# Placing in a sort kernel: the tile one-hot held still while both halves of the values stream past it

## What is computed

```
edge_index = jnp.stack([src, dst])
h = jnp.maximum(_layernorm(x, axis=-1), 0.0)
x = x + _L0_gnn_ref(h, edge_index, L0_gnn_kernel, L0_gnn_bias)
h = jnp.maximum(_layernorm(x, axis=-1), 0.0)
x = x + _L1_gnn_ref(h, edge_index, Wq, bq, Wk, bk, Wv, bv, gamma, beta)
# layer 0: sums = segment_sum(h[dst], by src); relu([mean, h] @ kernel + bias)
# layer 1: softmax attention of 8 heads over the edges of each src, then a layer norm
```

## Time and profile before

| what | us |
|---|---|
| median of 3 runs | 4550.31 |
| lowest and highest | 4537.21, 4554.0 |
| span of the profiled execution | 5884.4 |
| POOL busy, 55% of the span | 3217.7 |
| PE busy, 52% | 3071.8 |
| DVE busy, 52% | 3038.8 |
| ACT busy, 36% | 2089.2 |

### The profile page before, as it was taken

The page is one execution under the profiler, slowest core; times in us unless marked ns, Lnnn a source line. Parts: engine busy times, 40 slices in busy tenths (PEclk is TensorE's granted clock), DMA queues, the critical chain, the costliest instruction groups (busy, mean ns, idle before and its releaser), DMA issues. The chain is left out here.

```text
span 5884.4 us, 82972 instructions
## 1 busy us (share of the span) xinstructions
PE 3071.8 (52%) x19417; PEld 2269.0 (39%) x19417; DVE 3038.8 (52%) x8517; ACT 2089.2 (36%) x6025; POOL 3217.7 (55%) x3339
## 2 busy tenths in 40 slices
PE   4445445445445455354357555555555555555553
PEld 3324323334334333233234444444444444444442
DVE  7536446445345455354234555555555555555557
ACT  3233333433433333333344333333333333333333
POOL 3464464464564564554634555655555555555564
PEclk9556556556556556566557666666666666666665
DMA  2232232232222322322322333333333333333333
GB/s 80 63 82 53 70 80 55 73 79 55 76 72 56 81 68 57 84 62 61 87 57 68 101 103 100 106 101 102 104 101 105 102 101 105 101 104 103 100 105 63
DMA packets 245464, 490.01 MB, mean 83 GB/s; under 512 B 73156, under 2 KB 155197, under 8 KB 245022
## 3 DMA queue, kind: packets, MB, share of 16 engines
q0 software_dynamic: 153968, 371.50, 24.5%
q1 hardware_dynamic: 90350, 112.89, 6.9%
q10 hardware_dynamic: 704, 0.33, 0.0%
HBM read 468.15 MB, written 56.11 MB: 89 GB/s over the span
## 5 line engine op out<-in xcount | busy, mean ns | idle before, releaser
L533 POOL DMA_INDIRECT got<-hk_table,dst x1563 | 1561.2, 999 | 1325.5 <-PE bank L1003 647.5
L1513 POOL DMA_INDIRECT kv<-kv_table,dst_i x1611 | 1523.0, 945 | 1062.8 <-DVE wv_s L1554 611.4
L765 DVE TENSOR_TENSOR acc<-acc,bank 128x129 f32 x2187 | 634.2, 290 | 1250.2 <-remote 640.9
L1001 PE MATMUL bank<-got,oh 128*128 x2187 | 609.3, 280 | 1170.6 <-DVE acc L765 627.0
L1658 PE MATMUL bank<-q,ohT 128*128 x4833 | 757.8, 263 | 878.4 <-issue 574.6
L1572 DVE TENSOR_TENSOR acc<-acc,bank 128x136 f32 x1611 | 465.4, 289 | 1130.0 <-remote 1070.7
L1669 PE MATMUL bank<-wv_s,oh_f 128*128 128x136 f32 x3222 | 806.6, 401 | 255.5 <-issue 251.1
L1658 PEld LDWEIGHTS bank<-q,ohT 128*128 128x128 bf16 x4833 | 487.9, 101 | 1124.5 <-issue 1018.6
L1104 ACT ACTIVATE oh<-away 128x384 bf16<-128x384 bf16 x733 | 383.1, 523 | 1321.9 <-remote 784.1
L1669 PEld LDWEIGHTS bank<-wv_s,oh_f 128*128 128x128 f32 x3222 | 660.0, 282 | 344.0 <-issue 336.1
L1001 PEld LDWEIGHTS bank<-got,oh 128*128 128x128 bf16 x2187 | 239.9, 110 | 1369.2 <-issue 1317.5
(11 more groups left out here) (223 smaller groups left out, 3344.4 us busy)
## 6 DMA issues: line engine op xcount, KB each, us to landing
lane_r<-lane_of_slot SPq DMA_DIRECT2D x269, 192.0 KB
slots_by_bin<-sorted_chunk SPq DMA_DIRECT2D x637, 61.0 KB
kv<-kv_table,dst_i POOLq DMA_INDIRECT x1611
got<-hk_table,dst POOLq DMA_INDIRECT x1563
kv_table<-qkv SPq DMA_DIRECT2D x12, 512.0 KB, 2.9
hk_table<-hk POOLq DMA_DIRECT2D x6, 772.0 KB, 5.3
out<-o SPq DMA_DIRECT2D x12, 256.0 KB
xs<-in_x SPq DMA_DIRECT2D x3, 768.0 KB, 9.7
```

The source lines that it names most:

```text
L533: g.indirect_dma_start(out=got[:, (tile0[k] + t) % RING0, :], out_offset=None, in_=hk_d, in_offset=bass.IndirectOffsetOnAxis(dst0[:, k % 2 ...
L765: v.tensor_tensor(out=o, in0=o, in1=total0(u)[:, i * W0:(i + 1) * W0], op=ALU.add)\
L1001: t.matmul(o, w, row(2 * D, 3 * D + 1), start=True, stop=False)
L1513: g.indirect_dma_start(out=kv[:, r, i, :], out_offset=None, in_=kv_d, in_offset=bass.IndirectOffsetOnAxis(dst_i[:, t:t + 1], 0))\
```

## The change

`place` makes one matmul per column in place of two: `oh_t` becomes the stationary operand, and both halves of `val`, 256 columns, are the moving one. The result lies the other way round: tiles down the partitions, places across. So `vv` is already what `vT` needs, and `keep` takes it from `vv`. The row numbers of the gathers need the turned form: `dst0` is now made in a new function `destinations`, from what `turn` left in `bank[2]`, at `stage_at(n, 1)`, behind `add` of group 31.

```diff
                     v.scalar_tensor_tensor(out=vv[:, :], in0=bank[4][:, P:2 * P], scalar=1024.0, in1=low[:, :],
                                            op0=ALU.mult, op1=ALU.add).then_inc(s_v, 1)
-                    v.wait_ge(s_v, k + 1)
-                    c.inc(v.tensor_copy(v_i[:, :], vv[:, :]))
+
+                def destinations(k):
+                    v.wait_ge(s_vt, k + 1)
+                    c.inc(v.tensor_copy(v_i[:, :], bank[2][:, 256:256 + P]))
                     after(v, c)
                     v.tensor_scalar(out=dst0[:, k % 2, :], in0=v_i[:, :], scalar1=8191, scalar2=None,
                                     op0=ALU.bitwise_and).then_inc(s_dst, 1)
...
                 slots(0)
+                destinations(0)
                 incidences(0)
...
                         if n and g == stage_at(n, 0):
                             slots(k)
+                        if n and g == stage_at(n, 1):
+                            destinations(k)
...
                     for j in range(b - a):
-                        for l in range(2):
-                            ins = t.matmul(bank[4][:, l * P:(l + 1) * P],
-                                           val[:, q % 2, l * BLK:(l + 1) * BLK, :, j].rearrange("p w j -> p (w j)"),
-                                           oh_t[:, q % 2, j, :], start=(a == j == l == 0),
-                                           stop=(b == tiles_of(k) and j == b - a - 1 and l == 1))
+                        ins = t.matmul(bank[4][:, 0:2 * P], oh_t[:, q % 2, j, :],
+                                       val[:, q % 2, :, :, j].rearrange("p w j -> p (w j)"),
+                                       start=(a == j == 0), stop=(b == tiles_of(k) and j == b - a - 1))
                     ins.then_inc(s_plc, 1)
...
                 def keep(k):
-                    a.wait_ge(s_vt, k + 1)
+                    a.wait_ge(s_v, k + 1)
                     if k == 0:
                         a.wait_ge(s_zero, 16 * 5)
                     a.activation(vT[:, k, :].rearrange("p (j w) -> p w j", w=BLK),
-                                 bank[2][:, 256:256 + P].rearrange("p (w j) -> p w j", j=JS), ACT.Copy).then_inc(s_vTs, 1)
+                                 vv[:, :].rearrange("p (w j) -> p w j", j=JS), ACT.Copy).then_inc(s_vTs, 1)
```

## The result

The changed kernel takes 4592.38 us (median of 4 runs, 4587.92 to 4593.86), the kernel before 4552.16 us (4 runs, 4537.21 to 4558.64). The ratio is 1.0086, with a 95% interval of 1.0073 to 1.0099: slower by 40 us, outside the range of 4525 to 4580. Rival 1, the strided moving operand, had been priced at 4590 us and given a chance of 0.08.

The account below looks back on a forecast made before the run. POOL's issue of gathers was taken to bound both loops. The terms 0 + 0 + 0 + 0 + 0 + 0.8 us on 4550.3 gave 4551 us, range 4525 to 4580.

Parts of the forecast that it names:

- Rival 1: Strided streaming in placing makes PE the bound: 3.3 us a chunk, 40 us in all, 4590 us; chance 0.08.
- POOL's issue of gathers bounds both loops: In both layers' loops POOL's gathers set the time; at most 99 us of its waits are left in a plain run.
- the sum: POOL's time without waits inside the loops, 126 + 2030 + 16 + 184 + 2006 + 89 = 4451 us.
- That the stops of the earlier trace are the profiler's own: DVE's 132 "remote" stops of up to 8.7 us, and POOL's 132 waits beside them, come from the profiler.
- The moving operand 12 bytes apart: In `place`, strided reading costs PE 0 to 0.35 us a step, upper bound 2.56; on the path 0.
- The cover, 0.9 us of PE in a step and 9 us of margin in each chunk: In the sort PE has 0.9 us spare per step; POOL finishes a ring round 9 us later than other engines.
- Halving the matmuls gains nothing: In `place`, 6 matmuls of 256 columns take as long as 12 of 128: gain 0 to 0.07 us a step.
- Row numbers later, and DVE's wait for the turn: Row numbers still ready 10.3 us ahead; DVE waits 0.5 us or so per chunk, 6 us in all; cost 0.
- rival 3: Row numbers come too late for each chunk's first gather: up to 46 us slower, 4597 us; chance 0.03.
- `keep`: gain 0: ACT's `keep` no longer waits 1.5 to 1.9 us for the turn, but later groups wait for POOL: gain 0.
- Rivals 2 and 3: First of these: the bubble at `keep` was on the path, 23 us off, 4527 us, chance 0.09; other: rival 3.
- Chunk 0: +0.8 us: In chunk 0 `dst0` stays ahead, but DVE's work up to group 16 comes later: 0.8 us, once.

Follow-up runs that it names:

- b_again: The kernel before, unchanged, run again for a second profile: 4555.36 us (one run).
- micro: No computation, only bursts of 40 matmuls with operand elements 2 to 32 bytes apart: 256 moving columns take 0.109 us at 2 bytes, 0.340 at 12.
- fast_oh_n: The changed kernel with oh_t laid out columns innermost, a stationary operand at 12 bytes, on a chip of 4550 us: 4556.84 us, ratio 0.9996 to the kernel before.
- dummy4: The kernel before with four more contiguous 256-column matmuls in each full placing step, into columns nobody reads: 4563.76 us, ratio 1.0030.
- contig_n: The changed kernel with a contiguous moving operand, so sorted values are wrong, row numbers masked, on a chip of 4550 us: 4559.22 us, ratio 1.0005 to before.
- order_only: The kernel before with only the row numbers moved to group 34, behind PE's turn: 4554.05 us, ratio 1.0005.
- bf42: The kernel before with the moving one-hot in pieces of four and two columns, columns innermost, 8 and 4 bytes apart: 4505.78 us, ratio 0.9888.
- mix42: The changed kernel with oh_t columns innermost and val in pieces of four and two columns, 8 and 4 bytes apart: 4521.94 us, ratio 0.9923 to before.
- fast_oh: The changed kernel with oh_t laid out columns innermost, a stationary operand at 12 bytes, on the slower chip: 5987.79 us, ratio 1.0062 to the kernel before.
- contig: The changed kernel with a contiguous moving operand, so sorted values are wrong, row numbers masked, on the slower chip: 5922.75 us, ratio 0.9944 to before.

## Why the prediction was wrong

*POOL's issue of gathers bounds both loops: held.* The whole difference is found along POOL. Most of what the sum left, 99 us against the median and 102.6 against the span of `b_again`, has a name: a plain run's gather of layer 0 takes 1.040 us and not the 0.999 of the earlier trace rows, 64 us in all, and POOL waits 44 us at the tiles 64; the loop of layer 0 as a whole is 115 us longer than the sum's 2030, the rest of the kernel 13 us shorter. *That the stops of the earlier trace rows are the profiler's own: not borne out.* `b_again` records the same 82972 instructions without them, so the span does not stretch with the number of recorded instructions, and on the slower chip the runs without profiler take 5950 us as well. The prediction's sum over POOL did not depend on whose they are, but the claim was argued from a pattern alone.

*The moving operand 12 bytes apart: the step that failed, in its price.* It was taken at 0 to 0.35 us a step and at no cost on the path. It measured 0.23 us for each 256 columns at the faster clock and 0.13 at the slower, or, by the steps of the traces, 1.4 and 0.7 us a step. The end of the bounds, 2.56 us, was close; the value taken came from the loading of the same operand as the stationary side, as the nearest row. That row is of another kind: `micro` and `fast_oh_n` show that a stationary operand at 12 bytes costs nothing that can be seen, while a moving one at 12 bytes takes three times as long at the faster clock. The load's 124 against 95 ns said nothing of the price. The rule of the Trainium skill that was weighed (Advanced Engine Details and Errata, SBUF Cachelines) pointed to the right side, and `micro` differs from it in the form: with two hits on a 16-byte line, 8 bytes should be free, and they double the time (0.226 us against 0.109).

*The cover, 0.9 us of PE in a step and 9 us of margin in each chunk: the step that failed, on the path.* With the right price and this cover the forecast would still have been near 0: the full step, 2.2 us, stands exactly at the point from which rival 1 was to decide. The margin was worked out for chunk 5 alone, from a stretched trace. In `b_again` it is below zero in half of the chunks: POOL waits 6.2 to 7.8 us at tile 64 in six of twelve, and close to nothing in the others. So no cover was there in these, and part of any delay comes through; `dummy4` shows it at +0.6 us a step, 13 us. Why the waits alternate from chunk to chunk is open. Of the 20 steps x 0.7 to 1.4 us = 14 to 28 us that PE got longer in each chunk, (109.7 - 59.6) / 12 = 4.2 us reached POOL, so most of it is covered still; rival 1's 3.3 us a chunk was a choice inside 0 to 8, and it fits by that much luck.

*Halving the matmuls gains nothing: held.* `contig_n`, 1.0005 (0.9996 to 1.0014).

*Row numbers later, and DVE's wait for the turn: held in sum, mis-sized in the wait.* `order_only`, 1.0005. The last row number is ready at 982.76 + 0.23 = 982.99, the last gather of chunk 4 ends at 996.38:

```profile
982.43 0.29 DVE L661 CAST v_i<-bank 128x128 int32<-128x128 f32 x1 [5.23 <-PE bank L970]
...
982.76 0.23 DVE L663 TENSOR_SCALAR dst<-v_i 128x128 int32<-128x128 int32 x1
...
995.43 0.95 POOL L533 DMA_INDIRECT got<-hk_table,dst  x1 [0.30 <-issue]
...
996.68 0.95 POOL L533 DMA_INDIRECT got<-hk_table,dst  x1 [0.30 <-issue]
```

13.4 us ahead, where 10.3 were expected, and the next chunk's first gather stands only 0.30 us behind the one before. DVE's cast waits 3.9 us in the mean (50.3 / 13), not half a us: here 5.23. What it delays has cover. (In rival 3 the 4.2 us less cover and the 46 us do not go together: 46 is 12 x 3.8.) *`keep`: gain 0, held*; ACT's wait at that place fell from 137.3 us to 45.6, and nothing came of it in `contig_n`, which has it. Rivals 2 and 3 did not occur: `order_only` rules out the third by itself, and `contig_n`, where both could act, the second.

*Chunk 0: +0.8 us.* The first gather starts 4.2 us later than in `b_again` (130.49 against 126.29). `order_only` alone has it at 129.38 and `contig_n` at 126.28, though both make the row numbers late: some 3 us of this vary between builds, and how much of the 4.2 us is the change's own was not separated.

## What to carry to other kernels

When a matmul's two sides are exchanged, ask first how far apart the elements of the new moving operand lie: here the side that is loaded once could be strided at no cost, the side that streams only up to 4 bytes, and a row of one is no price for the other. A margin of one chunk is not the margin of all: take the wait at the same place in every chunk, and from a profile whose span is that of the runs. And an operation on one engine can shorten another engine's, as the one-hot's layout did the gathers; such an effect shows in the other's mean duration, not in its waits and not in its median.

## What the hardware showed that was not expected

**Streaming a strided moving operand.** For fp16, 256 columns take 0.109, 0.114, 0.172, 0.226 and 0.284 us at 2, 4, 6, 8 and 10 bytes at 2.4 GHz, 0.340 at 12 bytes at either clock, and 0.396, 0.452, 0.449 and 0.460 at 14, 16, 24 and 32 bytes at 1.2 GHz (`micro`). The kernel after has the same at 12 bytes (a step of 2.20 us throughout). A stationary operand at 12 bytes shows no such cost.

**DVE's writing and POOL's gathers.** With the columns innermost the one-hot takes 0.55 us for 768 elements against 0.95, and POOL's gathers in the same loop take 1.001 to 1.004 us in the mean instead of 1.032 to 1.040 (`fast_oh_n`, `bf42`, `mix42`), 44 to 60 us in 1563 of them. The median stays at 0.946 to 0.949; what shrinks are the gathers that meet a step's DVE instructions, from 1.248 us in the mean (`b_again`) to 1.137 (`fast_oh_n`) and 1.128 (`bf42`). What the two engines share there was not tested.

**A chip on which the engines stop.** On one chip all kernels took 5920 to 6050 us where they otherwise take some 4550, with and without the profiler, with stops on DVE, ACT and POOL that no instruction of the program ended. Ratios kept neither their size nor their sign there: `fast_oh` has 1.0062 (1.0044 to 1.0080) and on the other chip 0.9996 (0.9987 to 1.0005), `contig` 0.9944 (0.9927 to 0.9962) and 1.0005 (0.9996 to 1.0014).
